# Keys projected at step 10 and output projections at steps 30 and 31; attention values normalised as three chunks and then one

## What is computed

```python
def layernorm(x): return (x - mean(x)) / sqrt(var(x) + 1e-5)

q = (layernorm(x) @ Wq.T + bq).reshape(b, LQ, G, HPG, HD).transpose(0, 2, 3, 1, 4)   # 8 groups x 4 heads of 16
k = (ctx @ Wk.T + bk).reshape(b, LKV, G, HD).transpose(0, 2, 1, 3)
v = (ctx @ Wv.T + bv).reshape(b, LKV, G, HD).transpose(0, 2, 1, 3)
scores = einsum('bgrqd,bgkd->bgrqk', q, k) / sqrt(HD)      # masked by rows and by padding
out = einsum('bgrqk,bgkd->bgrqd', softmax(scores), v)
x = x + tanh(g_xattn[0]) * (out.reshape(...) @ Wo.T + bo)
x = x + tanh(g_ffn[0]) * moe(layernorm(x))                 # top 2 of 8 experts, and a shared expert
```

## Time and profile before

| | us |
|---|---|
| median of 3 runs (788.91 to 790.8) | 790.79 |
| the profiled execution's own time | 796.48 |
| its span, first to last instruction | 794.1 |
| mean granted clock of TensorE | 0.886 |
| PE busy | 690.3 |
| DVE busy | 439.8 |
| ACT busy | 292.2 |
| POOL busy | 110.4 |

### The profile page before, as it was taken

One profiled execution on the slowest core, in us unless ns is written; L12 is line 12 of the kernel. 1 busy time (PEld: TensorE's weight loads), 2 busy tenths in 40 slices (PEclk: granted clock), 3 DMA queues, 4 the chain that ended last, 5 costly groups with the idle time before them and its releaser, 6 DMA issues. The chain is left out here.

```text
span 794.1 us, 14865 instructions
## 1 busy us (share of the span) xinstructions
PE 690.3 (87%) x4399; PEld 481.3 (61%) x4417; DVE 439.8 (55%) x1017; ACT 292.2 (37%) x601; POOL 110.4 (14%) x144
## 2 busy tenths in 40 slices
PE   3488898998998998998999899897276999999997
PEld 2466566776776776876787676565163444444443
DVE  3275765675665656567568466543043555555554
ACT  2114644444434434444444443433012333333332
POOL 5500031112102202102102100311220000000000
PEclk9859679989988988999998898689587999999999
DMA  4647454845635535544463633445360122112211
GB/s 161 171 114 230 121 135 150 173 134 175 152 78 164 143 92 177 132 119 145 140 141 97 175 81 79 107 75 144 92 119 28 35 66 66 56 43 66 66 55 38
DMA packets 70982, 90.12 MB, mean 113 GB/s; under 512 B 13736, under 2 KB 47400, under 8 KB 70696
## 3 DMA queue, kind: packets, MB, share of 16 engines
q1 hardware_dynamic: 67512, 83.21, 37.7%
q0 software_dynamic: 2304, 6.29, 4.3%
q10 hardware_dynamic: 1136, 0.23, 0.1%
HBM read 60.48 MB, written 35.00 MB: 120 GB/s over the span
## 5 line engine op out<-in xcount | busy, mean ns | idle before, releaser
L644 ACT ACTIVATE probs<-ps 128x512 f32<-128x512 f32 x256 | 147.8, 598 | 149.2 <-PE ps L989 148.3
L863 DVE TENSOR_REDUCE mx<-ps 128x2 f32<-128x512 f32 x256 | 172.1, 684 | 47.4 <-PE ps L970 46.8
L970 PE MATMUL ps<-kst,qst 65*128 65x256 f32 x512 | 127.6, 337 | 15.5 <-DVE mx L863 9.4
L970 PEld LDWEIGHTS ps<-kst,qst 65*128 65x128 f32 x512 | 100.2, 218 | 62.8 <-issue 32.4
L989 PE MATMUL ps<-qst,kst 66*128 66x512 f32 x256 | 117.2, 460 | 23.8 <-ACT probs L644 23.5
L1142 PE MATMUL ps_h<-w,q_sg 128*128 128x512 bf16 x503 | 132.0, 383 | 6.0 <-PEq L77 5.6
L1193 DVE SCALAR_TENSOR_TENSOR hid<-ps_h,sc_in,up 128x256 bf16<-128x256 f32 x128 | 61.9, 484 | 87.2 <-ACT up L1183 86.2
L1183 ACT ACTIVATE up<-ps_h,sc_in 128x256 f32<-128x256 f32 x128 | 60.8, 475 | 120.1 <-PE ps_h L1142 120.1
L1142 PEld LDWEIGHTS ps_h<-w,q_sg 128*128 128x128 bf16 x512 | 49.9, 99 | 67.9 <-issue 10.4
L1002 PE MATMUL psa<-probs,v_st 128*32 128x256 f32 x1024 | 84.2, 455 | 1.2 <-ACT probs L644 1.2
L1160 PE MATMUL ps_o<-probs,hidT 128*128 128x512 bf16 x247 | 74.3, 380 | 1.4 <-DVE hidT L1199 0.8
(11 more groups left out here) (121 smaller groups left out, 1071.5 us busy)
## 6 DMA issues: line engine op xcount, KB each, us to landing
qst<-q_d SPq DMA_DIRECT2D x32, 384.0 KB
q_d<-q_sg SPq DMA_DIRECT2D x32, 256.0 KB, 3.2
a_d<-a_sb SPq DMA_DIRECT2D x32, 256.0 KB, 3.0
x_n<-in_x SPq DMA_DIRECT2D x8, 512.0 KB, 4.1
c_raw<-in_ctxT SPq DMA_DIRECT2D x8, 512.0 KB, 5.3
q_d<-q_sg SPq DMA_DIRECT2D x32, 128.0 KB, 4.8
a_dn<-a_d SPq DMA_DIRECT2D x16, 256.0 KB
a_lo<-r_d SPq DMA_DIRECT2D x16, 256.0 KB
```

The costliest lines, as they stand in the source:

```text
L644: act.activation(probs[:, v % 8, :], ps2[v % 2][:, :, :].rearrange("p h q -> p (h q)"), ACT.Exp, scale=HD ** -0.5).then_inc(s_exp, 1)
L863: dve.tensor_reduce(mx[:, c % 2, 0:8 * NT].rearrange("p (h t) -> p h t", t=NT)[:, h:h + 2, w // 2], ps1[u % 2][:, :, :], AX_X, ALU.max)\
L970: last = pe.matmul(o[:, i, :], qst[0:ROW_MAX, c, h, t * P:t * P + P], kst[0:ROW_MAX, c, g % 2, :], start=(i == 0 or not masked), stop=not ...
```

## The change

Four things are edited. **K** goes from step 13 to step 10, ahead of T0 and T1 (`FIRST` keeps the old order for the preparation before batch 0), and its stores go to step 12, ahead of the load of the residual (`load_residual`), which goes from step 12 to 16. **W0 and W1** go from steps 29 and 30 to 30 and 31, and DVE's second LayerNorm output of the batch (`norm2`, tile 1) from step 0 to step 1. **The two halves become two parts** `PART = ((0, 3), (3, 4))`: three chunks (384 KB tiles of 128 x 768 floats) and one (128 KB). **Their steps**: reciprocal of the first part 4 to 11, `load_values` and `store_r` 5 to 11, `load_r` 9 to 13, ACT's high part 16 to 21; of the second part only ACT's high part moves, 27 to 26. POOL multiplies the first part later in its list, and adds the residual before the low part.

```diff
-PREP = [(11, "T0"), (12, "T1"), (13, "K"), (14, "Q0"), (17, "Q1"), (20, "Q2"), (22, "Q3"), (25, "V0"), (26, "V1")]
+FIRST = ["T0", "T1", "K", "Q0", "Q1", "Q2", "Q3", "V0", "V1"]
+PREP = [(10, "K"), (11, "T0"), (12, "T1"), (14, "Q0"), (17, "Q1"), (20, "Q2"), (22, "Q3"), (25, "V0"), (26, "V1")]
...
-TAIL = [(0, "MT3"), (29, "W0"), (30, "W1")]
+TAIL = [(0, "MT3"), (30, "W0"), (31, "W1")]
...
+        PART = ((0, 3), (3, 4))
...
             def load_values(b, h):
 
-                for i in range(2):
-                    ready((s_aw[i], b * 32 + 16 * h + 16))
+                ready((s_aw[0], b * 32 + 32), (s_aw[1], b * 32 + 16 * h + 16))
                 ready((s_ln2, b * LN2))
-                sp.dma_start(a_dn[:, 2 * h:2 * h + 2, :].rearrange("p c q -> p (c q)"),
-                             a_d[b, :, 0:HD, 2 * L * h:2 * L * h + 2 * L]).then_inc(s_ar[h], 16)
+                c, end = PART[h]
+                sp.dma_start(a_dn[:, c:end, :].rearrange("p c q -> p (c q)"),
+                             a_d[b, :, 0:HD, L * c:L * end]).then_inc(s_ar[h], 16)
...
             def load_r(b, h):
-                ready((s_rw, b * 64 + 32 * h + 32), (s_ln2, b * LN2))
-                sp.dma_start(f(a_lo[:, 2 * h:2 * h + 2, :].rearrange("p c q -> p (c q)")),
-                             r_d[b, h].unsqueeze(1).broadcast_to([G, HD, 2 * L])).then_inc(s_rr[h], 16)
+                ready((s_rw, b * 64 + 48 + 16 * h), (s_ln2, b * LN2))
+                c, end = PART[h]
+                sp.dma_start(f(a_lo[:, c:end, :].rearrange("p c q -> p (c q)")),
+                             r_d[b, :, L * c:L * end].unsqueeze(1).broadcast_to([G, HD, L * (end - c)])).then_inc(s_rr[h], 16)
...
-                    if u == 12 and prev:
+                    if u == 12 and nxt:
+                        store_k(b + 1, idx)
+                    if u == 16 and prev:
                         load_residual(b - 1)
                     if u == 18 and old:
                         store_scores(b - 2)
-                    if u == 14 and nxt:
-                        store_k(b + 1, idx)
                     if u == 14 and attn:
                         load_stack(b, 3)
-                    if prev and u in (5, 19):
+                    if prev and u in (11, 19):
                         load_values(b - 1, u // 19)
-                    if prev and u in (5, 19):
                         store_r(b - 1, u // 19)
-                    if prev and u in (9, 21):
+                    if prev and u in (13, 21):
                         load_r(b - 1, u // 21)
...
-                if prev:
-                    normalise(b - 1, 0)
-                    low_values(b - 1, 0)
                 if attn:
                     values(b, 3, None)
                 if prev:
+                    normalise(b - 1, 0)
                     residual_bias(b - 1)
-                if prev:
+                    low_values(b - 1, 0)
                     normalise(b - 1, 1)
                     low_values(b - 1, 1)
...
-                    if u in (16, 27) and prev:
-                        h = u // 27
+                    if u in (21, 26) and prev:
+                        h = u // 26
...
-                    if u in (4, 19) and prev:
+                    if u in (11, 19) and prev:
                         h = u // 19
...
+                    if u == 1 and old:
+                        norm2(b - 2, 1)
...
-                    if u == 0 and old:
-                        norm2(b - 2, 1)
```

More of the change, by code:

```diff
@@ L92, in attention_phase @@
         a_d = dram("a_d", (B, G, 32, CH * L))
-        r_d = dram("r_d", (B, 2, G, 2 * L))
+        r_d = dram("r_d", (B, G, CH * L))
         def pair(name, cols):
@@ L263, in passes @@
         def passes(eng, body, prepare):
-            prepare(0, {name: k for k, (_, name) in enumerate(PREP)}, 0)
+            prepare(0, {name: k for k, name in enumerate(FIRST)}, 0)
             body(0, True, True, False, False, N_PREP, N_PREP % 2)
@@ L356, in move_sums @@
             def move_sums(b, c):
-                ready((s_aev, b * G + 2 * c + 2), (s_rd, b * 2 + c // 2 - 1))
+                ready((s_aev, b * G + 2 * c + 2), (s_rd, b * 2 + c // 3 - 1))
                 for w in range(2):
@@ L519, in normalise @@
                 pool.wait_ge(s_ar[h], b * 16 + 16)
-                half = a_dn[:, 2 * h:2 * h + 2, :]
-                pool.tensor_tensor(half, half, a_lo[:, 2 * h:2 * h + 2, :].bitcast(F32), ALU.mult).then_inc(s_an, 1)
+                c, end = PART[h]
+                part = a_dn[:, c:end, :]
+                pool.tensor_tensor(part, part, a_lo[:, c:end, :].bitcast(F32), ALU.mult).then_inc(s_an, 1)
             def low_values(b, h):
                 pool.wait_ge(s_ahi, b * 2 + h + 1)
-                pool.tensor_tensor(a_lo[:, 2 * h:2 * h + 2, :], a_dn[:, 2 * h:2 * h + 2, :],
-                                   a_hi[:, 2 * h:2 * h + 2, :].bitcast(F32), ALU.subtract).then_inc(s_alo, 1)
+                c, end = PART[h]
+                pool.tensor_tensor(a_lo[:, c:end, :], a_dn[:, c:end, :], a_hi[:, c:end, :].bitcast(F32), ALU.subtract)\
+                    .then_inc(s_alo, 1)
             def residual_bias(b):
@@ L654, in prepare @@
                 high_weight(0, 0)
-                for _, name in PREP:
+                for name in FIRST:
                     if name == "K":
@@ L666, in body @@
                         item(name, nb, idx[name], (par0 + par[name]) % 2, idx)
-                    if u in (16, 27) and prev:
-                        h = u // 27
+                    if u in (21, 26) and prev:
+                        h = u // 26
+                        c, end = PART[h]
                         act.wait_ge(s_an, b * 2 - 2 + h + 1)
-                        act.activation(a_hi[:, 2 * h:2 * h + 2, :], a_dn[:, 2 * h:2 * h + 2, :], ACT.Copy)\
-                            .then_inc(s_ahi, 1)
+                        act.activation(a_hi[:, c:end, :], a_dn[:, c:end, :], ACT.Copy).then_inc(s_ahi, 1)
                     if u == 7 and old:
@@ L870, in body @@
                         norm1(b + 1, u - 9)
-                    if u in (4, 19) and prev:
+                    if u in (11, 19) and prev:
                         h = u // 19
-                        for i in range(2):
-                            dve.wait_ge(s_den[i], b * 64 - 64 + 32 * h + 32)
-                        wait(dve, s_rw, b * 64 - 128 + 32 * h + 32)
-                        dve.reciprocal(rden[64 * h:64 * h + 64, :], den[64 * h:64 * h + 64, :]).then_inc(s_rd, 1)
+                        row, end = 32 * PART[h][0], 32 * PART[h][1]
+                        dve.wait_ge(s_den[0], b * 64)
+                        dve.wait_ge(s_den[1], b * 64 - 32 + 32 * h)
+                        wait(dve, s_rw, b * 64 - 80 + 16 * h)
+                        dve.reciprocal(rden[row:end, :], den[row:end, :]).then_inc(s_rd, 1)
                     if u in (6, 7) and old:
```

5 lines of the change are left out of this document (2 added, 3 removed).

## The result

| kernel | median, us | executions, us | ratio to before (95%) |
|---|---|---|---|
| before | 790.79 | 788.91 to 792.74 | |
| changed | 813.71 | 807.96 to 816.36 | 1.028 (1.0218 to 1.0342) |

What follows compares the result with a forecast made beforehand. PE, busy 690.3 of 794.1 us, was taken to bound the kernel through its idle stretches and slow clock. Batches 2 to 6 +13.2, the others +1.0, +2.3, -2.5, tail -0.5: +13.5 us, 804 on the median, range 778 to 813.

Steps and rivals of the forecast that it cites:

- slower as forecast: Whole kernel: the added load delays the sums and the time is 798 to 811 us; chance 0.50.
- K's stores: SP's stores before ACT's Q1: issued at 241.4, ACT's wait falls from 4.27 to about 2 us, PE's 3.48 to 1.
- The sums: Chunk 3's sums, awaited by DVE's reciprocal: land 3.4 us later, at 256.3 in batch 3; bounds 0 and 4.5.
- How they are delayed: Sums' issue to reciprocal, 6.15 us against 2.32 in the tail: some 4 us are a queue of earlier transfers.
- PE, +1.5 and +1.5 us a batch: PE's step 22 scores start 1.5 us later, and slow clock on the work after them costs another 1.5 us.
- W0: First output projection on PE: its 0.34 us wait goes in five batches, and its 1.96 us in batch 1.
- Batch 0 and 1: Batch 0 gains 2.5 us by earlier K's stores; batch 1 loses 1.0, being 3.0 less W0's wait of 1.96.
- Batch 7 and tail: Batch 7, without K, pays three quarters of 3.05 us, +2.3; the tail gains 0.5 us.
- faster: Whole kernel: the sums don't queue behind the added load, 773 us, or 781 with half of it; chance 0.28.
- break-even: Step 22 on PE: no loss if the sums land 1.9 us later than before, near 254.9 in batch 3.
- Slower still: Second part late too, ACT standing at step 26 with the exponentials behind, 1.5 us in six batches: 813; chance 0.10.
- same: Sums land 2 us later, slow stretch as before, steps 17 and 20 trade waits: 790 us, within 0.3%; chance 0.12.

Runs made afterwards that it cites:

- the extra load: Kernel before with K and output projections moved, plus an unneeded 384 KB load issued ahead of chunk 3's sums: 783.3 us, 0.9881.
- the version with K early: Kernel before with K at step 10, its stores at 12, the residual at 16, and output projections at steps 30 and 31: 770.0 us, 0.9712.
- The run with ACT's own queue: Changed kernel with chunk 3's two moves of sums issued by ACT through its own DMA queue instead of by SP: 808.1 us, 1.0213.
- The run with K's stores first: Changed kernel with K's two stores issued at step 11, ahead of the first part's load and stores of reciprocals: 826.6 us, 1.042.
- the residual's 7.8 us: Kernel before with K and output projections moved, and the residual's load behind the sums: 777.8 us, 7.8 us slower than with it ahead.
- the late steps: Kernel before with the first part's later steps but two halves: 796.9 us, 1.005; with K and output projections moved too: 801.8 us, 1.0106.
- the extra load behind the sums: Kernel before with K and output projections moved, plus an unneeded 384 KB load at step 17 behind chunk 3's sums: 800.0 us, 1.0073.

## Why the prediction was right, and where its sizes were off

The forecast was slower, 804, in 778 to 813; the chain named (added load, later sums, PE idle at step 20, then a slow clock) is what the trace shows. The number was at the edge: the median of 813.71 is 0.7 us above the range, and by the ratio, 1.028, the time is 812.9, just inside. It is above the 798 to 811 of "slower as forecast". The median is 9.4 us above the sum's 804.3. Of that 6.8 are between the two profiled executions and the medians (16.1 against 22.9); 2.6 are the sum (13.5 predicted, 16.1 measured).

- **K's stores.** Predicted at 241.4, ACT's wait about 2, PE's about 1. Measured 242.35 in a batch that begins 1.82 later, so 240.5 in the time of before; 2.13 and 1.34. Right.
- **The sums.** Predicted 3.4 us later, from 3.05 of transfer and 0.4 of start. In batch 3 the reciprocal starts at 255.96 instead of 252.99, 1.15 later in the batch's own time; the mean of batches 2 to 6 is 2.5 later, 0.8 by a later issue and 1.8 by a longer lag, where the sum had 0.4 and 3.05. The cost itself was right: the extra load added about 3 us where nothing else changed. The step that failed is the one that left the rest of the queue as it is now: against the version with K early the lag is 3.9 us more (7.52 against 3.66), against the kernel before only 1.4 (6.15), since moving K and the residual takes 2.5 off it.
- **How they are delayed.** I read the 6.15 us against 2.32 as a queue of earlier transfers. The run with ACT's own queue shows that it is no queue behind SP's other transfers alone: the lag is the same from either queue, and most of it, 5.0 of 7.75 us in batch 3, passes before the sums' first piece. The residual, 512 KB taken from ahead of them, gave 0.6 us of lag where 207 GB/s would give 2.5. So the size came near, but not by that rule.
- **PE, +1.5 and +1.5 us a batch.** The maximum of step 22 comes 0.35 later, not 1.5, that of step 24 another 2.4 later instead of the 1.5 of the slow clock. Together 2.7, against 3.0. The total over batches 2 to 6 was 11.8 against 13.2: right in part by luck, by two errors of opposite sign, and uneven: batches 2 and 5 have 9.0 of the 11.8.
- **Q0's stores.** No term of the sum. ACT's Q2 waits 24.8 us for them in batches 1 to 6, and not at all before. The wait ends 1.2 to 1.8 us ahead of the sums', so it is covered by theirs, but it bounds what earlier sums can give back.
- **W0.** Its wait in the batches is gone, as predicted (the 1.96 us of batch 1 too, for which the earlier trace rows name no releaser); alone, the move is worth nothing (1.0003).
- **Batch 0 and 1**: -3.8 and +2.2, predicted -2.5 and +1.0. Small, opposite.
- **Batch 7 and tail**: +6.2, predicted +1.8. This is the term of the sum that was mis-sized most. I gave the sums of batch 7 only three quarters of a transfer. The trace of batch 7 after:

```profile
503.33 2.15 SPq L377 DMA_DIRECT2D r_d<-rden  x3
...
508.60 0.66 SPq L382 DMA_DIRECT2D a_lo<-r_d  x1
...
511.08 1.20 SPq L364 DMA_DIRECT2D den<-a_sb  x2
...
519.21 0.55 DVE L879 RECIPROCAL rden<-den 32x64 f32<-32x64 f32 x1 [8.07 <-DMA den<-a_sb]
520.54 0.80 PE L973 MATMUL ps<-kst,qst 65*128 65x256 f32 x2 [5.82 <-DVE mx L865]
```

There are no stores of K to issue here, so SP stands 3.1 us before `a_lo` for the landing of the reciprocals, and the sums are issued 34.7 us into the batch instead of 31.6: late by SP's wait, and then lagging 8.1 instead of 5.6. I had counted what SP issues ahead of the sums, but not, in batch 7, what it waits for. The run with K's stores first shows such a wait in every batch.

What the changed profile was to show: `k_d` at half of 35.6 (19.5), `den` over 40 us (53.1), the second reciprocal 8 us behind the issue (6.4 to 9.5), the slow clock behind step 20, W0 without a wait; all there. One lag, 6.45 us in batch 2, is just under the 6.5 that was named as a sign of being wrong; the others are above. The prediction set a figure beside the faster rival that needs its condition: the Trainium skill, DMA: Bandwidth & Descriptors, "Anatomy of one DMA", gives the 2 us and 436 GB/s for transfers that GpSimd issues. These are issued by SP. The rival *faster* needed the sums to land less than 1.9 us later than now. In the mean of batches 2 to 6 they were 2.5 later, and it fell. In batch 3 they were only 1.15 later, on its side of the break-even, and PE even started the scores of step 22 0.84 us earlier in the batch's own time (257.29 less 1.82, against 256.31), yet the batch took 0.9 us longer. My break-even priced the start of step 22 alone; the loss lies behind it, in the work that runs at half clock. *Slower still* forecast 813, near the median, but not by its mechanism: the second part was not late (ACT's high parts in batch 3 have no idle time before them). The *same* fell.

What stays open: why the medians differ by 22.9 us and the profiled executions by 16.1, since only one execution of each is traced. The one before seems to be the odd one: the run with the output projections alone moved measures like before (1.0003), its trace has 789.2 us of span, and against it the changed kernel takes 21.1 us more, 2.7 a batch in batches 2 to 6 instead of 2.4. Open too are where the rest of the residual's 7.8 us lies, and what holds back a small transfer before its first piece moves.

## What to carry to other kernels

Where two waits end within 2 us of each other, price an edit with the other wait taken away: the late steps cost 0.5% behind K's wait (1.005) and 32 us without it, and sums that came earlier met the wait for Q0's stores just behind. A load moved ahead of a small transfer that someone waits for delays it, here by 3 us for 384 KB and 13 us of time. So try each part of a change by itself before the whole (K's move alone, 0.976, beats the whole change by 42 us; with the output projections it measured 0.9712, whose interval meets that of K alone). On a queue issued in order look for the waits for a landing between two issues: each holds back all that stands behind it. An experiment can bring in such a wait of its own, as the extra load behind the sums did: look at the issue times before you blame the bytes.

## What the runs showed of the hardware

- Two 4 KB transfers issued together take 2.3 us from the first issue to use when the engines are free (2.29 in batch 7 from ACT's queue, 2.32 in the tail before) and 6.4 to 9.5 us in batches 1 to 6 of the changed kernel (in batch 3, 2.07 MB are moved in the 7.5 us), from either of two queues: a queue of its own did not let them pass.
- From the queue of their own their first piece starts 5.0 us after the issue in batch 3, and 1.2 in batch 7.
- 384 KB ahead of them on eight groups of partitions cost about 3 us of lag.
- Less waiting on one engine is not time: 29 us less of DVE's waits for the sums gave 5.6 us, 9 us less from the residual's move in the changed kernel gave 11.4.
